# Two blocks of TensorE's stream change places in an attention kernel: the turn of the maxima and the sums of a group

## The chip, the cores and the metric

One core of a Trainium2 chip runs the whole kernel. The metric is the time of one execution on the device in microseconds; the median of several executions counts.

## What is computed

A gated block in two parts, for 16 sequences of 512 tokens with 512 features, in fp32. The first part is attention with 16 heads of 32 features, causal, of the normalised x over a context; the second is a channel mix (three matrix products with a shift by one token, a squared relu and a sigmoid).

```python
def _xattn(Q, K, V, mask, Wq, bq, Wk, bk, Wv, bv, Wo, bo):
    q, k, v = heads(Q @ Wq.T + bq), heads(K @ Wk.T + bk), heads(V @ Wv.T + bv)
    scores = jnp.einsum('bhqd,bhkd->bhqk', q, k) * SCALE
    scores = jnp.where(mask[:, None, None, :] == 0, -jnp.inf, scores)
    scores = jnp.where(causal[None, None], scores, -jnp.inf)
    attn = jax.nn.softmax(scores, axis=-1)
    return merge(jnp.einsum('bhqk,bhkd->bhqd', attn, v)) @ Wo.T + bo

x = x + jnp.tanh(g_xattn[0]) * _xattn(_layernorm(x), ctx, ctx, mask, ...)
x = x + jnp.tanh(g_ffn[0]) * _ffn(_layernorm(x), W_r, W_k, W_v, mu_r, mu_k)
```

## The kernel before, in words

The attention phase goes through 256 slots, one for each head of each sequence (16 slots a sequence, called a batch here), and 14 more to run out. `slot(i)` exists for each engine, and each engine runs through its own list of slots; semaphores alone tie them together. Several heads are in flight at once.

In slot i, TensorE does for head i the scores of the queries against the keys (`scores`, L844), in three portions: s0 (two products of 128 and 256 columns), s1 (384) and s2 (512), in two PSUM banks by turns. VectorE reads each portion and takes the maximum of each row (`maximum`, L697, four a slot). After an odd slot it splits the eight columns of maxima of two heads in a high and a low part (`split_maxima`, L705 and L707). In the even slot behind, TensorE turns them from columns to rows (`turn_maxima`, L853, a transpose into the bank `sum_ps`), ScalarE copies them out (`copy_maxima`, L518), and SP moves them by DMA into two rows of the stack `q_stack` (`stack_maxima`, L305).

With them TensorE makes, three slots behind, for head u = i - 3, the transposed scores less their maxima (`probabilities`, L867), again in three portions, p0, p1 and p2 (512, 384 + 128 and 256 columns), in two banks by turns. ScalarE takes their exponential (`exponent`, L531, three a slot) into a ring `probs` of five heads; GpSimd masks them (L383, L387) and adds them up in part (L394, L397).

Four heads are a group. In every fourth slot, from slot 8 on, TensorE makes the values of a group (`values`, L884, 32 products whose weights have 32 columns; four heads lie side by side in the columns of the array) and its sums, with ones as weights (L889, L892, L895, such products too, into `sum_ps`). The last of them raises `values_done`. In this document such a slot, i = 4m, is a group slot. The turn and the sums use the same bank: the sums wait until ScalarE has copied the turned maxima out (`max_copied`), and a turn waits until VectorE is through with the sums before (`refined`).

Behind `values_done` comes, in the order of ScalarE's list: the first exponential of the group slot (its place in the ring is the one that the values have just read), the logarithm of the sums (`log_sums`, L538), the second exponential, the reciprocal by an exponential of the negative logarithm (`invert_sums`, L542), the third exponential. VectorE then corrects the reciprocal (`refine`, L713 and L715), at the end of its list for the group slot, so ahead of the maxima of the next slot, and there scales the values (`normalise`, L720).

Between all these lie the projections of q, k, v and the output, each product split in three of high and low parts (`exact_product`, L54 to L56). A table written out by hand, `WORK`, says for each of the 16 slots of a batch which steps stand in each of three parts, where one step is three products of 512 columns:

```python
0: ("", "q1 2", ""),            # group slot; 4 and 8 alike, 12: ("", "q0+ 01", "")
1: ("q1 3,k1 0", "k1 12", "k1 3"),
2: ("v2 01", "v2 23", "v3 0"),  # 6 and 14 alike; 10: ("x0+", ...), four transposes
```

The waits of TensorE that matter here are written in the kernel as counts:

```python
# scores(u, c)
pe.wait_ge(scores_read, T * u + (-1, 0, 2)[c])
# probabilities(u, c)
pe.wait_ge(exp_done, 3 * u + c - 1)
# exponent(u, c), on ScalarE
act.wait_ge(values_done, (u - RING) // HG + 1)
```

So s2 of head u waits for two maxima of the same head, and p0, p1 and p2 wait for the exponential two portions earlier.

SP issues all DMA in one list: the stacks of q and k for later slots (L280, L289), the maxima (L305), loads of x, context and residual, and stores. The channel mix (from about 1475 us on) has lists of its own and isn't part of what is described here.

Of the kernel before, what the change touches and what calls it, by code (L numbers as in the profile page):

```python
# [83 lines left out]
def attention_phase(nc, lent, x, ctxT, mask, g_xattn, wqT, bq, wkT, bk, wvT, bv, woT, bo, x1, mask_bias, ffn_wT):  # L84
# [13 lines left out]
    HG = P // DH  # L98
    N = B * H
    LAG = 3  # L100
    VALUES = 8
# [14 lines left out]
    with ExitStack() as ctx:  # L116
# [130 lines left out]
        def k_stack_count(G):  # L247
            b, g = divmod(G, K)
            return 112 * b + (64 if g < 2 else 112)

        def value_block(b, g):
            return 0 if g < 2 else 1 + b % 2
# [579 lines left out]
        def _(pe):  # L832
            def scores(u, c):
                G, j = divmod(u, HG)
                n = G % 2
                if c == 0 and u % 2 == 0:
                    pe.wait_ge(q_stacked[n][j // 2], 48 * (G // 2 + 1))
                    pe.wait_ge(k_stacked[n][j // 2], k_stack_count(G))
                if u > 0 or c == 2:
                    pe.wait_ge(scores_read, T * u + (-1, 0, 2)[c])  # L840
                here = score_ps[(3 * u + c) % 2]
                for t in ((0, 1), (2,), (3,))[c]:
                    at = P if t == 1 else 0
                    last = nc.tensor.matmul(here[:, at:at + P * (t + 1)], q_stack[n][0:MASK_ROW + 1, j, P * t:P * t + P],  # L844
                                            k_stack[n][0:MASK_ROW + 1, j, 0:P * (t + 1)], start=True, stop=True)
                last.then_inc(scores_done, 1)

            def turn_maxima(q):
                pe.wait_ge(max_split, q + 1)
                ended = (2 * q + 1 - VALUES) // HG + 1  # L850
                if ended > 0:
                    pe.wait_ge(refined, ended)
                nc.tensor.transpose(sum_ps[0:2 * PAIR * T, 0:P], split_max[:].bitcast(F32), ident[:]).then_inc(max_turned, 1)  # L853

            def probabilities(u, c):

                G, j = divmod(u, HG)
                n = G % 2
                if c == 0 and u % 2 == 0:
                    pe.wait_ge(max_stacked[n][j // 2], 16 * (G // 2 + 1))  # L860
                if 3 * u + c >= 2:
                    pe.wait_ge(exp_done, 3 * u + c - 1)
                here = prob_ps[(3 * u + c) % 2]
                at = 0
                for k in PT_SETS[c]:
                    width = S - P * k
                    last = nc.tensor.matmul(here[:, at:at + width], k_stack[n][0:ROWS, j, P * k:P * k + P],  # L867
                                            q_stack[n][0:ROWS, j, P * k:S], start=True, stop=True)
                    at += width
                last.then_inc(probs_done, 1)  # L870

            def values(G):

                b, g = divmod(G, K)
                pe.wait_ge(summed, 2 * HG * (G + 1))
                pe.wait_ge(v_copied, T * (b + 1))
                if G > 0:
                    pe.wait_ge(normalised, G)
                if g == 1 and b + 1 < B:
                    pe.wait_ge(xt_low, T * (b + 2))  # L880
                for k in range(T):
                    for j in range(HG):
                        at = P * (g % 2) + DH * j
                        nc.tensor.matmul(value_ps[DH * j:DH * j + DH, P * k:S], v[:, value_block(b, g), k, at:at + DH],  # L884
                                         probs[:, (HG * G + j) % RING, PT_AT[k]:PT_AT[k] + S - P * k],
                                         start=(k == 0), stop=(k == T - 1), skip_group_check=True)
                pe.wait_ge(max_copied, min(2 * G + 4, N // 2))
                for j in range(HG):
                    nc.tensor.matmul(sum_ps[DH * j:DH * j + DH, 0:P], ones[:], probs[:, (HG * G + j) % RING, 0:P],  # L889
                                     start=True, stop=True, skip_group_check=True)  # L890
                for j in range(HG):
                    nc.tensor.matmul(sum_ps[DH * j:DH * j + DH, P:S], ones[:], prob_sum[:, (HG * G + j) % RING, :],  # L892
                                     start=True, stop=False, skip_group_check=True)
                for j in range(HG):
                    last = nc.tensor.matmul(sum_ps[DH * j:DH * j + DH, LATE:S], ones[:],  # L895
                                            probs[:, (HG * G + j) % RING, PT_AT[3]:PT_AT[3] + P],
                                            start=False, stop=True, skip_group_check=True)
                last.then_inc(values_done, 1)
# [51 lines left out]
            def transpose_x(b, m):  # L950
                if m != 1:
                    free_bank(f"x{m}", b)
                elif b > 0:
                    pe.wait_ge(normalised, K * (b - 1) + 1)
                pe.wait_ge(ln_applied, T * b + m + 1)
                for k in range(K):
                    last = nc.tensor.transpose(bank(f"x{m}")[:, P * k:P * k + P], tiles[:, m, P * k:P * k + P], ident[:])
                last.then_inc(xt_done, 1)
# [3 lines left out]
            def work(b, s, part):  # L962
                for piece in WORK[s][part].split(","):
                    if not piece:
                        continue
                    name, *steps = piece.split()
                    of = b + {"+": 1, "-": -1}.get(name[2:], 0)
                    if not 0 <= of < B:
                        continue
                    if name[0] == "x":  # L970
                        transpose_x(of, int(name[1]))
                    for k in (steps[0] if steps else ""):
                        project[name[0]](of, int(name[1]), int(k))

            def slot(i):
                b, s = divmod(i, H)
                u = i - LAG
                now, then = 0 <= i < N, 0 <= u < N
                if now:
                    scores(i, 0)  # L980
                if then:
                    probabilities(u, 0)
                if 2 <= i <= N and i % 2 == 0:
                    turn_maxima(i // 2 - 1)
                if i % HG == 0 and 0 <= i - VALUES < N:
                    values((i - VALUES) // HG)
                work(b, s, 0)
                if now:
                    scores(i, 1)
                if then:  # L990
                    probabilities(u, 1)
                if now:
                    scores(i, 2)
                work(b, s, 1)
                if then:
                    probabilities(u, 2)
                work(b, s, 2)
# [16 lines left out]
            for i in SLOTS:  # L1014
                slot(i)
# [439 lines left out]
```

## Time and profile before

| | |
|---|---|
| median of 3 runs | 2069.2 us (2066.35 to 2071.6) |
| the profiled execution | 2069.11 us |
| its span, first to last instruction | 2067.4 us |
| busy: TensorE, VectorE, GpSimd, ScalarE | 1943.2, 1355.8, 1298.9, 975.5 us |
| TensorE's granted clock over the span | 0.979 |

Read it so: TensorE is busy for 94% of the span, no other engine for more than 66%. The clock is given as a share of full speed. Idle time of the other engines costs nothing as long as TensorE doesn't wait for them; so the table alone doesn't tell what bounds a slot, the order of events does. Busy times of TensorE are those of pipelined products whose ends are modelled: the distance from start to start tells more than a length.

### The profile page before, as it was taken

The numbers are of one execution on the slowest core, as the hardware profiler recorded it, in microseconds if no ns is written. First come the engines' busy times: TensorE is split into PE (matmuls) and PEld (weight loads), VectorE is DVE, ScalarE is ACT, GpSimd is POOL, SyncE is SP. The second block draws the span as 40 slices with busy tenths as digits, with TensorE's granted clock in tenths as the row PEclk, the third lists the DMA queues.
The fourth block names the chain that finished last, engine by engine and source line by source line (L and its number), as shares of the span: only waits on it lengthen the run. The fifth ranks groups of instructions, "written<-read, shape, count | busy, mean of one in ns | idle before, by whom it ended". The sixth has DMA issues, their size and how long they took to land. (4 is left out here: it accounts for less than half of the span.)

```text
span 2067.4 us, 36565 instructions
## 1 busy us (share of the span) xinstructions
PE 1943.2 (94%) x11648; PEld 1499.7 (73%) x11648; DVE 1355.8 (66%) x3534; ACT 975.5 (47%) x1869; POOL 1298.9 (63%) x1829
## 2 busy tenths in 40 slices
PE   4999999999999999999999999994599999999999
PEld 3677777777777777777777777772388888888887
DVE  3776677766777767767677676765457566666663
ACT  3555555555555555555555454544233343434342
POOL 4566666666666666666666666556267777777770
PEclk9999999999999999999999999996799999999999
DMA  5545455454644545545554455443121313232221
GB/s 180 114 114 129 109 153 116 111 126 114 149 119 107 125 121 144 116 113 123 125 142 112 119 119 129 118 115 98 61 82 66 117 61 106 76 101 81 89 74 62
DMA packets 128665, 229.31 MB, mean 111 GB/s; under 512 B 18656, under 2 KB 20704, under 8 KB 127616
## 3 DMA queue, kind: packets, MB, share of 16 engines
q1 hardware_dynamic: 128512, 227.43, 42.2%
q8 instruction: 77, 1.26, 0.3%
q14 instruction: 76, 0.62, 0.1%
HBM read 92.06 MB, written 33.59 MB: 61 GB/s over the span
## 5 line engine op out<-in xcount | busy, mean ns | idle before, releaser
L697 DVE CUSTOM_DVE_ANT_0 score_ps<-score_ps,causal 128x128 f32<-128x128 f32 (+3 forms) x1024 | 489.2, 505 | 342.2 <-PE score_ps L844 340.8
L531 ACT ACTIVATE probs<-prob_ps 128x512 f32<-128x512 f32 (+1 forms) x768 | 399.2, 528 | 404.6 <-PE sum_ps L895 202.2
L844 PE MATMUL score_ps<-k_stack,q_stack 97*128 97x128 f32 (+3 forms) x1024 | 319.7, 353 | 20.8 <-DVE least L697 13.7
L867 PE MATMUL prob_ps<-q_stack,k_stack 100*128 100x512 f32 (+3 forms) x1024 | 284.7, 319 | 14.3 <-ACT probs L531 7.2
L383 POOL TENSOR_SCALAR_AFFINE_SELECT probs<-probs 128x256 f32<-128x256 f32 x256 | 110.2, 430 | 277.6 <-ACT probs L531 277.6
L394 POOL TENSOR_TENSOR prob_sum<-probs 128x384 f32<-128x384 f32 x256 | 261.2, 1020 | 0.0
L844 PEld LDWEIGHTS score_ps<-k_stack,q_stack 97*128 97x128 f32 x1024 | 188.9, 191 | 72.5 <-DVE least L697 30.8
L867 PEld LDWEIGHTS prob_ps<-q_stack,k_stack 100*128 100x128 f32 x1024 | 193.1, 192 | 37.7 <-DMA q_stack<-max_rows 9.5
L397 POOL TENSOR_TENSOR prob_sum<-prob_sum,probs 128x256 f32<-128x256 f32 x256 | 194.6, 760 | 36.7
L387 POOL TENSOR_SCALAR_AFFINE_SELECT probs<-probs 128x256 f32<-128x256 f32 x256 | 106.4, 415 | 175.6 <-ACT probs L531 175.5
L884 PE MATMUL value_ps<-probs,v 128*32 128x512 f32 (+3 forms) x2048 | 155.1, 444 | 12.3 <-POOL prob_sum L397 12.3
L1129 POOL TENSOR_SCALAR wk_low_room<-wk_low_room,ffn_moments,ffn_newton 128x512 f32<-128x512 f32 x56 | 163.6, 2930 | 2.9 <-POOL ffn_newton L80 2.8
L1148 POOL TENSOR_TENSOR kact_low<-square,kact_high 128x512 fp32r<-128x512 f32 x64 | 82.1, 1306 | 120.2 <-ACT kact_high L1196 120.2
L1286 DVE SCALAR_TENSOR_TENSOR square<-ffn_k_ps,relu 128x512 f32<-128x512 f32 x64 | 44.3, 692 | 160.0 <-ACT relu L1190 159.9
L697 DVE DVE_READ_ACCUMULATOR2_ANT least<- 128x1 f32 x1024 | 145.8, 142 | 0.0
L884 PEld LDWEIGHTS value_ps<-probs,v 128*32 128x32 f32 x2048 | 61.5, 111 | 103.4 <-issue 76.3
L54 PE MATMUL proj_ps<-cT_high,wk_high 128*128 128x512 f32 x256 | 102.2, 399 | 17.3 <-DVE wk_low L738 17.3
L1190 ACT ACTIVATE relu<-ffn_k_ps 128x512 f32<-128x512 f32 x64 | 38.3, 598 | 166.1 <-PE ffn_k_ps L56 166.1
L54 PE MATMUL ffn_k_ps<-mix_k_high,xT_high 128*128 128x512 f32 x256 | 105.6, 413 | 10.0 <-DVE mix_k_low L1272 10.0
L54 PE MATMUL proj_ps<-wo_high,attn_high 128*128 128x512 f32 x256 | 106.3, 415 | 8.0 <-issue 5.2
L54 PE MATMUL proj_ps<-wv_high,cT_high 128*128 128x512 f32 x256 | 104.5, 408 | 3.3 <-DVE xT_low L675 3.3
L54 PE MATMUL proj_ps<-xT_high,wq_high 128*128 128x512 f32 x256 | 102.2, 399 | 1.6 <-DVE staged_q_low L680 1.6
(144 smaller groups left out, 4879.7 us busy)
## 6 DMA issues: line engine op xcount, KB each, us to landing
k_stack<-staged_k_high SPq DMA_DIRECT2D x256, 128.0 KB
q_stack<-staged_q_high SPq DMA_DIRECT2D x256, 128.0 KB, 3.1
tiles<-in_x SPq DMA_DIRECT2D x16, 1024.0 KB, 5.6
k_stack<-staged_k_low SPq DMA_DIRECT2D x128, 128.0 KB
q_stack<-staged_q_low SPq DMA_DIRECT2D x128, 128.0 KB, 3.2
x_io<-in_x SPq DMA_DIRECT2D x16, 1024.0 KB, 6.9
x<-x_io SPq DMA_DIRECT2D x64, 256.0 KB, 3.3
wk_low_room<-x SPq DMA_DIRECT2D x16, 1024.0 KB, 5.6
```

The costliest lines, as they stand in the source:

```text
L54: nc.tensor.matmul(out, s_high, m_high, start=first and n == steps[0], stop=False)
L383: nc.gpsimd.affine_select(out=pair, in_=pair, compare_op=ALU.is_ge, fill=0.0, base=0, pattern=[[0, 2], [1, P]], channel_multiplier=-1).the ...
L387: nc.gpsimd.affine_select(out=pair, in_=pair, compare_op=ALU.is_ge, fill=0.0, base=0, pattern=[[0, 2], [1, P]], channel_multiplier=-1).the ...
L394: nc.gpsimd.tensor_tensor(total, here[:, P:S], here[:, PT_AT[1]:PT_AT[1] + LATE], ALU.add).then_inc(summed, 1)
L397: nc.gpsimd.tensor_tensor(total[:, P:LATE], total[:, P:LATE], here[:, PT_AT[2]:PT_AT[2] + 2 * P], ALU.add).then_inc(summed, 1)
L531: nc.scalar.activation(probs[:, u % RING, lo:hi], prob_ps[(3 * u + c) % 2][:, 0:hi - lo], ACT.Exp, scale=SCALE).then_inc(exp_done, 1)
L697: nc.vector.tensor_tensor_reduce(out=here, in0=here, in1=causal[:, LATE - P * t:S], scale=-1.0, scalar=3e38, op0=ALU.add, op1=ALU.min, acc ...
L844: last = nc.tensor.matmul(here[:, at:at + P * (t + 1)], q_stack[n][0:MASK_ROW + 1, j, P * t:P * t + P], k_stack[n][0:MASK_ROW + 1, j, 0:P ...
L867: last = nc.tensor.matmul(here[:, at:at + width], k_stack[n][0:ROWS, j, P * k:P * k + P], q_stack[n][0:ROWS, j, P * k:S], start=True, stop ...
L884: nc.tensor.matmul(value_ps[DH * j:DH * j + DH, P * k:S], v[:, value_block(b, g), k, at:at + DH], probs[:, (HG * G + j) % RING, PT_AT[k]:P ...
L1129: nc.gpsimd.tensor_scalar(x_in[:, m, :], x_in[:, m, :], moments[:, m, 0:1], newton[:, 1, m:m + 1], ALU.subtract, ALU.mult).then_inc(ln_app ...
L1148: nc.gpsimd.tensor_tensor(kact[1][:, k, :], square[:, k, :], kact[0][:, k, :].bitcast(F32), ALU.subtract).then_inc(kact_low, 1)
```

## The change

Two blocks change places in TensorE's list. The turn of the maxima stands behind the first share of projections of its even slot, or, in a group slot, where that share is empty, behind the values, instead of ahead of both. The sums of a group, a part of `values` before, become a function `sums` of their own, which is called behind s1, p1 and s2 instead of directly behind the values. No instruction is added or taken away, and the lists of the other engines stay as they are.

```diff
                         nc.tensor.matmul(value_ps[DH * j:DH * j + DH, P * k:S], v[:, value_block(b, g), k, at:at + DH],
                                          probs[:, (HG * G + j) % RING, PT_AT[k]:PT_AT[k] + S - P * k],
                                          start=(k == 0), stop=(k == T - 1), skip_group_check=True)
+
+            def sums(G):
+
                 pe.wait_ge(max_copied, min(2 * G + 4, N // 2))
                 for j in range(HG):
                     nc.tensor.matmul(sum_ps[DH * j:DH * j + DH, 0:P], ones[:], probs[:, (HG * G + j) % RING, 0:P],
...
                     scores(i, 0)
                 if then:
                     probabilities(u, 0)
+                grouped = i % HG == 0 and 0 <= i - VALUES < N
+                if grouped:
+                    values((i - VALUES) // HG)
+                work(b, s, 0)
                 if 2 <= i <= N and i % 2 == 0:
                     turn_maxima(i // 2 - 1)
-                if i % HG == 0 and 0 <= i - VALUES < N:
-                    values((i - VALUES) // HG)
-                work(b, s, 0)
                 if now:
                     scores(i, 1)
                 if then:
                     probabilities(u, 1)
                 if now:
                     scores(i, 2)
+                if grouped:
+                    sums((i - VALUES) // HG)
                 work(b, s, 1)
                 if then:
                     probabilities(u, 2)
```

## Rows read from the trace of the kernel before

**Rows 1.** Busy time by stretch: start:end, length, busy per engine, clock, DMA.

```profile
160.00:1420.00 1260.00, 1216.22 (x8191) 922.46 (x8193) 878.60 (x2656) 666.32 (x1325) 786.02 (x1250) 0.99 0.51 124
```

**Rows 2.** Waits from 160 to 1420 us: us in total, times, longest.

```profile
ACT probs L531 <- PE sum_ps L895: 186.0, 58, 3.3
...
PEld sum_ps L853 <- DVE split_max L707: 36.8, 48, 1.8
...
PEld score_ps L844 <- DVE least L697: 26.1, 59, 0.5
```

**Rows 3.** TensorE in time: start, length, operation, [idle before].

```profile
638.62 0.27 PE L853 MATMUL sum_ps<-ident,split_max 128*16 128x128 f32 x1
638.82 2.36 PE L884 MATMUL value_ps<-probs,v 128*32 128x512 f32 x32
641.00 0.40 PE L889 MATMUL sum_ps<-probs,ones 128*32 128x128 f32 x8
...
641.86 0.40 PE L895 MATMUL sum_ps<-probs,ones 128*32 128x128 f32 x8
642.19 0.45 PE L844 MATMUL score_ps<-k_stack,q_stack 97*128 97x384 f32 x1
...
643.00 0.39 PE L54 MATMUL proj_ps<-xT_high,wq_high 128*128 128x512 f32 x1
643.23 0.39 PE L55 MATMUL proj_ps<-xT_low,wq_high 128*128 128x512 f32 x1
...
644.11 0.48 PE L867 MATMUL prob_ps<-q_stack,k_stack 100*128 100x512 f32 x1
...
646.64 0.51 PE L844 MATMUL score_ps<-k_stack,q_stack 97*128 97x512 f32 x1 [0.26 <-DVE least L697]
```

**Rows 4.** ScalarE in time, the same group slot.

```profile
642.39 0.60 ACT L531 ACTIVATE probs<-prob_ps 128x512 f32<-128x512 f32 x1 [3.21 <-PE sum_ps L895]
...
643.36 0.60 ACT L531 ACTIVATE probs<-prob_ps 128x512 f32<-128x512 f32 x1
643.84 0.64 ACT L542 ACTIVATE inverse<-inverse 128x512 f32<-128x512 f32 x1
```

**Rows 5.** VectorE in time, the same group slot and the next.

```profile
644.51 0.70 DVE L713 TENSOR_TENSOR sum_ps<-sum_ps,inverse 128x512 f32<-128x512 f32 x1 [0.56 <-ACT inverse L542]
...
646.06 0.47 DVE L697 CUSTOM_DVE_ANT_0 score_ps<-score_ps,causal 128x256 f32<-128x256 f32 x1
```

**Rows 6.** TensorE in time around the turn, slots 2, 6, 12 and 14.

```profile
649.40 0.39 PE L867 MATMUL prob_ps<-q_stack,k_stack 100*128 100x512 f32 x1
650.80 0.28 PE L853 MATMUL sum_ps<-ident,split_max 128*16 128x128 f32 x1 [1.00 <-DVE split_max L707]
...
671.21 0.39 PE L867 MATMUL prob_ps<-q_stack,k_stack 100*128 100x512 f32 x1
671.90 0.28 PE L853 MATMUL sum_ps<-ident,split_max 128*16 128x128 f32 x1 [0.30 <-DVE split_max L707]
...
702.89 0.40 PE L867 MATMUL prob_ps<-q_stack,k_stack 100*128 100x512 f32 x1
703.38 0.28 PE L853 MATMUL sum_ps<-ident,split_max 128*16 128x128 f32 x1
...
715.39 0.40 PE L867 MATMUL prob_ps<-q_stack,k_stack 100*128 100x512 f32 x1
715.62 0.27 PE L853 MATMUL sum_ps<-ident,split_max 128*16 128x128 f32 x1
715.71 0.47 PE L54 MATMUL proj_ps<-wv_high,cT_high 128*128 128x512 f32 x1
```

**Rows 7.** Issues on SP in time, of slot 2: the maxima.

```profile
651.39 0.65 SPq L305 DMA_DIRECT2D q_stack<-max_rows  x1
```

**Rows 8.** DMA issues: operation, count, KB each, median us to landing.

```profile
q_stack<-staged_q_high SPq DMA_DIRECT2D x256, 128.0 KB, 3.1
...
mask_bias<-x_io SPq DMA_DIRECT2D x1, 32.0 KB, 1.6
```

## The prediction

> **What bounds the kernel now.** First the busy table by stretch. From 160 to 1420 us the kernel is in the steady part of the attention phase, and TensorE is busy in 1216.2 of 1260 us at a granted clock of 0.99, far ahead of the others [rows 1]. So only two things can move the time there: work added to or taken from TensorE's stream, and its gaps. The channel mix behind 1500 us isn't touched.
>
> Then the table of waits, for the gaps [rows 2]. TensorE's weight loads stood 36.8 us before the turned maxima (L853), 48 times, until VectorE had split them; that is what the change aims at. They also stood 26.1 us, 59 times, before a score product until VectorE had read earlier scores. 59 in 1260 us is once in four slots. And ScalarE waited 186.0 us, 58 times, 3.2 us each, for L895, the last sums of a group. That is once in four slots too, and it asks what hangs on those sums.
>
> Then one group slot in order of time. I count from z = 641.86, where the row of the last sums (L895) starts. TensorE: turn 638.62, values 638.82, sums 641.00, then s1, p1, s2 (scores 1, probabilities 1, scores 2) from 642.19 to 643.00, and the projections [rows 3]. ScalarE begins the group's first exponential at 642.39 = z + 0.53, when L895 is over; then logarithm, second exponential at 643.36 (0.60 long) and reciprocal at 643.84 (0.64 long) follow back to back, to 644.48 [rows 4]. VectorE waits for the reciprocal: its correction starts at 644.51, and only behind it comes the second maximum of the next slot, 646.06 to 646.53 [rows 5]. TensorE's s2 of that next slot needs it and starts at 646.64, after a gap that the row puts down to VectorE [rows 3]. **So from the sums to that s2 there is a fixed chain of 4.78 us (z to 646.64) over ScalarE and VectorE, and TensorE already waits at its end.** The next slot's p0 at 644.11 waits a little too: the second exponential, which frees its bank, ends at 643.96.
>
> **The change part by part.** Nothing is computed more or less; two blocks change places on TensorE.
>
> *Gain: the turn comes later.* In a slot 4m + 2 the six projection products (four transposes at slot 10) now stand ahead of the turn, in a slot 4m the values. From p0 to the turn is 0.23 us without a wait (715.39 to 715.62, slot 14), but 1.40 in slot 2, 0.69 in slot 6 and 0.49 in slot 12 [rows 6]. Saved: 1.17 + 0.46 + 0.26 = 1.89 us in a batch. The first and the last of the 16 batches have neither the same neighbours nor the same waits, so 15 count: **28.4 us**. Does the wait really end? In slot 2 the turn would be reached at 649.40 + 0.23 + 6 x 0.23 = 651.01; the split let it go at 650.80 [rows 6], 0.2 us before. Slots 6 and 12 have more room.
>
> *Cost: the sums come behind s1, p1, s2.* This block now lies ahead of z. Where it stood it took 0.81 us (642.19 to 643.00). At the spacing of a product with 512 columns, 0.23 us (643.00 to 643.23) [rows 3], its 384 + 512 + 512 columns would take 0.17 + 0.23 + 0.23 = 0.63; the other 0.18 is spent on getting out of the products with 32 columns of weights. The turn, before, took 0.20 to the values (638.62 to 638.82); ahead of s1 it should be near the 0.09 that it takes ahead of a projection [rows 3, 6]. I take 0.81 - 0.11 + 0.02 = **0.72 us** more from a group slot's start to z; the 0.02 is for one more switch, which no row shows by itself. Low end: 0.63 - 0.11 = 0.52. High end: the turn saves nothing, and going into the values and into the sums costs another 0.11 each, 0.81 + 0.22 = 1.03.
>
> Would the 0.72 be given back behind z, where the block is missing? **No: this is the step that decides.** TensorE would reach the next slot's p0 earlier, but the second exponential ends z + 2.10 as before, and s2 is let go z + 4.78 as before. ScalarE is idle before z and full from z + 0.53 to z + 2.6 either way. VectorE reads the maxima of s1 and s2 before z instead of behind it, but then waits for the same reciprocal. So the gap behind z grows by what the block took. Slot 12 has six projection products in the middle instead of three, but the same chain with a fourth link on ScalarE, so I count it alike. Group slots with scores behind them, and no transfer of the channel mix's weights ahead: 8, 12, ..., 248, that is 61. 61 x 0.72 = **43.9 us**.
>
> *What is queued behind the moved turn.* On ScalarE: copying the maxima, and behind that the slot's exponentials. In a slot 4m they wait for the sums anyhow; in 4m + 2 the first comes some 1.4 us later while the p2 that needs it has three to six products ahead of it: nothing. On GpSimd, masks and sums of the exponentials shift with them; values need them a slot later: nothing. The sums themselves wait for that copy. Turn to end of copy is about 0.6 us (650.80, and the transfer's issue at 651.39 [rows 6, 7]) while s1, p1, s2 lie between: 0.8, nothing. On SP's queue: the transfer of the maxima and, in 4m + 2, the K stack of the next group behind it, 1.4 us later but needed more than a slot later: nothing. The maxima's own transfer is tighter. In a slot 4m + 2 behind the turn stand s1, p1, s2 (0.63 to 0.81), nine products (2.07), p2 and the next s0 (0.3 together): p0 comes 3.0 to 3.2 us behind the turn, 2.4 to 2.6 behind the issue. No row shows the landing of these 8 KB; 32 KB to DRAM took 1.6 us, 128 KB to the same stack 3.1 [rows 8]. By size it is nearer the first: nothing, with up to 0.7 us a slot kept for a rival.
>
> *Sum.* 43.9 - 28.4 = **+15.5 us** on the profiled execution's 2069.1 us (span 2067.4 and 1.7 around it), which is the median of the runs (2069.2) to 0.1. **2084.6 us.** With the ends of the block's cost: 61 x 0.52 - 28.4 = +3.3 and 61 x 1.03 - 28.4 = +34.4, that is 2072 to 2103.
>
> *A rule against the row.* Behind the sums the block takes those 0.18 us more than its columns [rows 3]: a change from one kind of product to the other isn't free here. The Trainium skill, "TensorE: Matmul & The Clock Gate", section "Step-by-step: what each phase is for", says that weights are loaded while earlier products are in flight. By that rule the switches would be free and only the low end paid.
>
> **The rivals.** A measurement of this kernel tells about 0.3% (6.2 us) from no change.
>
> *Switches are hidden in the new places* (0.12): the low end, +3.3 us, 2072. For it: score loads between projections cost nothing now. Against it: the 0.18 us behind the sums. This is what the rule of the page named above would give.
>
> *Faster: the chain doesn't hang on the sums* (0.11). The place is VectorE's correction. If it is let go by something ahead of the sums, the moved block is taken out of TensorE's stream behind z and put in ahead at no loss, and only the 28.4 us stay, less 61 extra switches of 0.11: -21.7, 2047. It decides from the point where the correction starts earlier than z + 2.65; halfway is no change. For it: the turn's waits are large and plainly in the stream. Against: the logarithm reads the very bank that the sums write, and the code's exponential waits for the same count.
>
> *The maxima land late* (0.06). If the 8 KB need 3.1 us as the 128 KB do, p0 of the slot behind 4m + 2 waits 0.5 to 0.7, in three slots of a batch: 15 x 3 x 0.6 = +27 more, 2112.
>
> *The turn waits still* (0.04). VectorE is at its limit in slots 4m + 1; if half of the 28.4 stays, 2099.
>
> *The forecast* (0.67): the rest, 2073 to 2103, most of it over 2076.
>
> **How the numbers follow.** Slower by over 0.3%: 0.65 of the forecast, 0.05 of the hidden switches, 0.06 and 0.04: 0.80. Within 0.3%: 0.02, 0.07, and 0.03 of halfway: 0.12. Faster: 0.08. The range 2070 to 2101 takes the forecast with nearly all of its bounds, the hidden switches and the remaining wait, and leaves out the faster rival and the late maxima, under 2 in 10.
>
> **What the profile will show.** Right: no gap before the turn (L853) in slots 2, 6 and 12, and z about 4.5 us behind a group slot's start; z to the next slot's s2 still 4.8, with the waits of L844 for the maxima's reading (26.1 us now) up by some 35 to 45; ScalarE's wait for L895 up from 3.2 to about 4.5 us each. Wrong: a correction earlier than z + 2.65 (the faster rival), waits of L867 for the transfer from max_rows (late maxima), or waits of L853 that stay. A granted clock under 0.97 in the same stretch would be something that I haven't counted.

## The result, and the profile after

The changed kernel takes 2094.3 us (median of four runs, 2093.1 to 2094.9), the kernel before, beside it, 2067.8 us: ratio 1.0128, 95% interval 1.0115 to 1.014. **It is 26.5 us slower.** The forecast was +15.5 us, the range 2070 to 2101. The profiled execution's span is 2092.7 us, 25.3 more than before.

TensorE has as many instructions as before and the same share of busy time, 94%. The steady stretch of the attention, by stretch as in [rows 1]:

```profile
160.00:1420.00 1260.00, 1216.72 (x8095) 902.31 (x8094) 863.11 (x2615) 651.30 (x1304) 773.41 (x1236) 1.00 0.49 121
```

In the same time TensorE is as busy as before, 1216.7 against 1216.2 us, but gets through 8095 products instead of 8191. So busy time doesn't show the loss: a product that stands behind a wait or a switch has a longer row (0.50 us at 653.49 below, 0.39 to 0.40 for its neighbours). The waits from 160 to 1430 us (us in total, times, longest), to be held against [rows 2]:

```profile
DVE sum_ps L713 <- ACT inverse L542: 162.3, 58, 3.2
...
ACT probs L531 <- PE sum_ps L898: 101.5, 58, 1.8
...
PEld score_ps L844 <- DVE least L697: 34.6, 59, 1.0
...
PE prob_ps L867 <- ACT probs L531: 20.2, 44, 0.8
```

The turn's waits for the split are gone from the list. New is TensorE's wait for an exponential (L867), and VectorE's wait for the reciprocal is 2.8 us each, against 0.7 before (39.4 us in 58 waits): it reads the maxima ahead of it now and has nothing left to do. Now the same group slot as [rows 3 and 6], TensorE in order of time (start, length, operation, idle before); the sums have the lines L892, L895 and L898 here:

```profile
648.76 0.39 PE L867 MATMUL prob_ps<-q_stack,k_stack 100*128 100x512 f32 x1
...
649.08 2.36 PE L884 MATMUL value_ps<-probs,v 128*32 128x512 f32 x32
651.37 0.28 PE L853 MATMUL sum_ps<-ident,split_max 128*16 128x128 f32 x1
651.40 0.42 PE L844 MATMUL score_ps<-k_stack,q_stack 97*128 97x384 f32 x1
651.66 0.40 PE L867 MATMUL prob_ps<-q_stack,k_stack 100*128 100x384 f32 x2
651.90 0.44 PE L844 MATMUL score_ps<-k_stack,q_stack 97*128 97x512 f32 x1
652.27 0.42 PE L892 MATMUL sum_ps<-probs,ones 128*32 128x128 f32 x8
...
653.16 0.40 PE L898 MATMUL sum_ps<-probs,ones 128*32 128x128 f32 x8
653.49 0.50 PE L54 MATMUL proj_ps<-xT_high,wq_high 128*128 128x512 f32 x1
...
655.41 0.47 PE L867 MATMUL prob_ps<-q_stack,k_stack 100*128 100x512 f32 x1 [0.45 <-ACT probs L531]
...
657.94 0.50 PE L844 MATMUL score_ps<-k_stack,q_stack 97*128 97x512 f32 x1 [0.27 <-DVE least L697]
```

Two numbers are to be read off. From z, the start of the last sums (653.16), to s2 of the next slot (657.94) it is **4.78 us, to the hundredth what it was before** [rows 3]. And from p0 to z it is 4.40 us, against 3.47 before (0.23 from p0 to the turn [rows 6], then 638.62 to 641.86 [rows 3]): 0.93 more. Over the 62 group slots of each trace the medians are the same: p0 to z 3.47 before and 4.40 after, z to s2 4.78 in both. Behind slot 12 the chain is longer, 5.30 before and 5.29 after. The first exponential on ScalarE and the correction on VectorE:

```profile
653.69 0.60 ACT L531 ACTIVATE probs<-prob_ps 128x512 f32<-128x512 f32 x1 [1.75 <-PE sum_ps L898]
```

```profile
655.81 0.70 DVE L713 TENSOR_TENSOR sum_ps<-sum_ps,inverse 128x512 f32<-128x512 f32 x1 [2.67 <-ACT inverse L542]
```

The first exponential starts at z + 0.53, the correction at z + 2.65, as in [rows 4 and 5].

The slots' lengths, from the start of s0 to that of the next (median over twelve batches in the middle of the trace, us), with the mean length of a batch of 16, show where time went for this kernel and for all that follow (slots 3, 7, 11 and 15 stay within 0.04 us in all of them, slot 8 is like 0, and 5 and 9 are like 1 but for e1 and e6, where they are 5.38 and 4.90):

| kernel | 0 | 1 | 2 | 4 | 6 | 10 | 12 | 13 | 14 | batch |
|---|---|---|---|---|---|---|---|---|---|---|
| before | 5.64 | 5.38 | 6.03 | 5.65 | 5.40 | 5.61 | 6.63 | 5.87 | 4.92 | 86.7 |
| changed | 6.03 | 5.92 | 4.84 | 6.03 | 4.84 | 5.61 | 6.59 | 6.57 | 4.86 | 88.3 |
| e1 | 5.64 | 5.47 | 4.84 | 5.65 | 4.84 | 5.61 | 6.63 | 5.86 | 4.86 | 85.1 |
| e2 | 6.03 | 5.91 | 6.02 | 6.03 | 5.40 | 5.62 | 6.59 | 6.58 | 4.91 | 90.1 |
| e3 | 6.13 | 5.92 | 6.03 | 6.13 | 5.38 | 5.62 | 6.96 | 6.58 | 4.91 | 90.8 |
| e4 | 5.64 | 4.90 | 6.37 | 5.65 | 5.75 | 6.44 | 6.63 | 5.48 | 5.37 | 86.8 |
| e5 | 6.03 | 5.43 | 4.85 | 6.03 | 4.84 | 5.62 | 6.59 | 5.59 | 4.86 | 86.1 |
| e6 | 5.64 | 5.49 | 4.84 | 5.64 | 4.84 | 6.46 | 6.63 | 5.48 | 4.86 | 84.8 |
| e7 | 5.64 | 4.90 | 5.19 | 5.65 | 4.84 | 6.46 | 6.65 | 5.48 | 4.86 | 84.3 |
| e8 | 6.30 | 5.37 | 4.84 | 6.30 | 4.84 | 5.63 | 7.02 | 5.87 | 4.86 | 87.2 |
| e9 | 5.64 | 4.90 | 5.19 | 5.64 | 4.84 | 6.46 | 6.64 | 5.48 | 4.86 | 84.3 |
| e10 | 5.64 | 4.90 | 5.19 | 5.64 | 4.84 | 6.46 | 6.63 | 5.48 | 4.86 | 84.2 |
| e11 | 5.64 | 5.39 | 5.28 | 5.64 | 5.37 | 5.62 | 6.37 | 5.87 | 4.92 | 85.6 |
| e12 | 5.64 | 4.90 | 4.84 | 6.44 | 4.84 | 5.69 | 6.37 | 5.48 | 4.86 | 83.7 |

The change gains 1.19 us in slot 2, 0.56 in slot 6 and 0.06 in slot 14, and loses 0.92 to 0.93 in each pair of a group slot and the slot behind it (0 and 1, 4 and 5, 8 and 9), 0.66 in 12 and 13, where the turn's wait of 0.26 was inside.

### The profile page after: what moved, and what is told of

It is laid out like the page before. It is cut to its first block and busy times, and to the rows that moved or that the text cites. A ratio compares the mean times of both kernels' runs of the same rounds, so it can differ in the third digit from the quotient of the medians.

```text
span 2092.7 us, 36565 instructions
## 1 busy us (share of the span) xinstructions
PE 1961.2 (94%) x11648; PEld 1488.8 (71%) x11648; DVE 1354.7 (65%) x3534; ACT 972.4 (46%) x1869; POOL 1296.5 (62%) x1829
## 5 line engine op out<-in xcount | busy, mean ns | idle before, releaser
L531 ACT ACTIVATE probs<-prob_ps 128x512 f32<-128x512 f32 (+1 forms) x768 | 395.0, 527 | 271.3 <-PE prob_ps L867 158.7
L844 PE MATMUL score_ps<-k_stack,q_stack 97*128 97x128 f32 (+3 forms) x1024 | 320.1, 354 | 29.9 <-DVE least L697 14.8
L867 PE MATMUL prob_ps<-q_stack,k_stack 100*128 100x512 f32 (+3 forms) x1024 | 291.2, 325 | 34.9 <-ACT probs L531 28.0
L867 PEld LDWEIGHTS prob_ps<-q_stack,k_stack 100*128 100x128 f32 x1024 | 193.4, 192 | 74.7 <-issue 26.3
L844 PEld LDWEIGHTS score_ps<-k_stack,q_stack 97*128 97x128 f32 x1024 | 189.2, 191 | 71.9 <-DVE least L697 40.3
L397 POOL TENSOR_TENSOR prob_sum<-prob_sum,probs 128x256 f32<-128x256 f32 x256 | 194.6, 760 | 36.7
L713 DVE TENSOR_TENSOR sum_ps<-sum_ps,inverse 128x512 f32<-128x512 f32 x64 | 44.8, 700 | 195.4 <-ACT inverse L542 195.4
L518 ACT COPY max_rows<-sum_ps 16x128 f32<-16x128 f32 x128 | 32.5, 254 | 242.0 <-PE sum_ps L853 242.0
```

Of the source, the lines that this page charges most:

```text
L397: nc.gpsimd.tensor_tensor(total[:, P:LATE], total[:, P:LATE], here[:, PT_AT[2]:PT_AT[2] + 2 * P], ALU.add).then_inc(summed, 1)
L531: nc.scalar.activation(probs[:, u % RING, lo:hi], prob_ps[(3 * u + c) % 2][:, 0:hi - lo], ACT.Exp, scale=SCALE).then_inc(exp_done, 1)
```

## The experiments

The theory in one sentence: only the way from a group slot's start to its sums counts, because a chain of 4.8 us over ScalarE and VectorE hangs on them; and the turn's waits were really in TensorE's stream. Each run below takes one piece of it. The kernel before ran beside each of them, with medians of 2066.5 to 2067.0 us. An edit shifts the lines behind it by one or two, so L843 and L866 are in some of these kernels what L844 and L867 are before.

### The two parts of the change, each alone

**e1**, the turn late in slots 4m + 2, group slots untouched:

```diff
-                if 2 <= i <= N and i % 2 == 0:
+                if 2 <= i <= N and i % HG == 0:
                     turn_maxima(i // 2 - 1)
                 if i % HG == 0 and 0 <= i - VALUES < N:
                     values((i - VALUES) // HG)
                 work(b, s, 0)
+                if 2 <= i <= N and i % HG == 2:
+                    turn_maxima(i // 2 - 1)
```

> The kernel before with one part of the change: in the slots 4m + 2 the turn stands behind the first share of projections; the group slots stay as they were. Theory (the turn's waits were plainly in TensorE's stream, the loss came from the sums alone): slots 2, 6 and 14 are shorter by 1.19, 0.55 and 0.06 us as in the changed kernel, 1.80 us in each of 15 batches, 27 us in all, so about 2041 us, faster than both kernels. Rival (VectorE is the bound, and time won at the turn is lost again at the next group's correction or split): within 0.3% of the kernel before, with larger waits of the scores for the reading of the maxima.

Measured: 2043.9 us, ratio 0.9888 (0.9869 to 0.9906), **22.7 us faster than before**. The turn in slot 2 of this kernel:

```profile
640.90 0.40 PE L54 MATMUL proj_ps<-wv_high,cT_high 128*128 128x512 f32 x1
...
641.59 0.27 PE L853 MATMUL sum_ps<-ident,split_max 128*16 128x128 f32 x1
641.62 0.42 PE L844 MATMUL score_ps<-k_stack,q_stack 97*128 97x384 f32 x1
```

No idle time stands before the turn. Of the expected 27 us 4 are missing. Slot 1 has a wait in most batches that it didn't have before (waits of this kernel, 160 to 1400 us):

```profile
PEld prob_ps L867 <- DMA q_stack<-max_rows: 17.2, 16, 6.5
```

The longest of them, 6.5 us near the end of the attention phase, isn't new: the kernel before waits 6.3 us in the same slot. Of the other 15, 10.7 us in all, 13 are in slot 1, and slot 1 got longer in some batches: the maxima's transfer lands late there, which is one of the forecast's rivals in a single place. e7 comes back to it.

**e2**, the other part alone: as the changed kernel, with the turn of the slots 4m + 2 back ahead of the projections.

```diff
                 grouped = i % HG == 0 and 0 <= i - VALUES < N
+                if 2 <= i <= N and i % HG == 2:
+                    turn_maxima(i // 2 - 1)
                 if grouped:
                     values((i - VALUES) // HG)
                 work(b, s, 0)
-                if 2 <= i <= N and i % 2 == 0:
+                if 2 <= i <= N and i % HG == 0:
                     turn_maxima(i // 2 - 1)
```

> The other part of the change alone: in the group slots values, turn, s1, p1, s2, sums; in the slots 4m + 2 the turn stays ahead of the projections. Theory (fixed chain from the sums): 0.92 us more in 61 group slots, 0.26 less in 15 of them (the turn's wait in slot 12), +52 us, about 2120 us, and the waits before the turn in slots 2 and 6 stay at 1.0 and 0.3 us. Rival (only the extra switches on TensorE cost, some 0.3 us a group): +14 us, 2082 us.

Measured: 2120.7 us, ratio 1.0253 (1.0233 to 1.0272), +54 us. Parts and whole agree: 54 less the 27 that the slots of e1 gain is the change's 26.5; by e1's whole time, 22.7, it would be 31, and the transfer's waits in slot 1, of which the changed kernel has hardly any, stand between. The rival, switches alone, is out.

**e3**, the smaller edit: only the sums moved, all turns at their old places.

```diff
+                if 2 <= i <= N and i % 2 == 0:
+                    turn_maxima(i // 2 - 1)
                 grouped = i % HG == 0 and 0 <= i - VALUES < N
                 if grouped:
                     values((i - VALUES) // HG)
                 work(b, s, 0)
-                if 2 <= i <= N and i % 2 == 0:
-                    turn_maxima(i // 2 - 1)
```

> Only the sums moved behind s1, p1 and s2; all turns stay at their old places, ahead of the values. Theory: the way from a group slot's start to the sums is longer by the block (0.81 us) and about 0.1 for a switch, the chain behind them stays 4.8 us, 61 times: +55 us, about 2123 us. If the sums move costs clearly less than e2, the turn's new place behind the values is a cost of its own. Rival (switches alone): +6 to +15 us.

Measured: 2129.8 us, ratio 1.0298 (1.028 to 1.0317), +63 us, where +55 was expected, and 9 more than e2. The turn's place behind the values is a gain, not a cost: 0.10 us a group slot, and the wait of slot 12. The rows of a group slot show the price of each switch between the products with 32 columns of weights and the others:

```profile
664.37 0.39 PE L867 MATMUL prob_ps<-q_stack,k_stack 100*128 100x512 f32 x1
664.60 0.27 PE L853 MATMUL sum_ps<-ident,split_max 128*16 128x128 f32 x1
664.80 2.36 PE L884 MATMUL value_ps<-probs,v 128*32 128x512 f32 x32
667.09 0.44 PE L844 MATMUL score_ps<-k_stack,q_stack 97*128 97x384 f32 x1
667.38 0.40 PE L867 MATMUL prob_ps<-q_stack,k_stack 100*128 100x384 f32 x2
667.62 0.44 PE L844 MATMUL score_ps<-k_stack,q_stack 97*128 97x512 f32 x1
667.99 0.43 PE L892 MATMUL sum_ps<-probs,ones 128*32 128x128 f32 x8
...
668.87 0.40 PE L898 MATMUL sum_ps<-probs,ones 128*32 128x128 f32 x8
```

The values take 2.29 us to the next product (664.80 to 667.09) where they took 2.18 to the sums (638.82 to 641.00 [rows 3]): 0.11 for leaving the products with 32 columns of weights. s2 takes 0.37 to the sums (667.62 to 667.99) against 0.29 to a projection (642.71, where s2 began before, to 643.00): 0.08 for entering them. p0 to z is 4.50 us (664.37 to 668.87), 1.03 more than before; 61 times that is 62.8 us.

### Where the chain is held

**e4**, the kernel before, with VectorE's correction moved from ahead of the next slot's first two maxima to behind them. TensorE's list isn't touched.

```diff
-                if i % HG == 0 and 0 <= i - VALUES < N:
-                    refine((i - VALUES) // HG)
...
                 if i % HG == 1 and 0 <= i - VALUES < N:
+                    refine((i - VALUES) // HG)
                     normalise((i - VALUES) // HG)
```

> The kernel before with VectorE's correction of the reciprocal moved behind the first two maxima of the next slot, directly ahead of the scaling of the values; nothing on TensorE changes. Theory (s2 of the slot behind a group slot waits only because the correction stands ahead of two maxima): the gap of 0.42 us before that s2 is gone, 61 times, 20 to 26 us faster, 2042 to 2048 us; z to that s2 falls from 4.8 to about 4.35 us. Rival (the chain is bound on ScalarE or by VectorE's whole load, the order there doesn't matter): no change, and the waits turn up before the turn in slots 2 and 6.

Measured: 2069.4 us, ratio 1.0012 (1.0002 to 1.0022): **no gain**, if anything 0.1% slower. Theory and rival were each half right. The gap before s2 is gone everywhere (slot 1 from 5.38 to 4.90, slot 13 from 5.87 to 5.48), so s2 does wait because of the correction's place in the list. But slots 2, 6, 10 and 14 are longer by as much, as the rival had it. Its waits from 160 to 1420 us:

```profile
PEld sum_ps L852 <- DVE split_max L707: 70.3, 72, 1.8
...
PEld score_ps L843 <- DVE least L697: 0.5, 2, 0.4
```

26.1 us before the scores became 0.5, and 36.8 us before the turn became 70.3 [rows 2]. Counted from z, VectorE ends its split of the slot behind a group slot at the same time in either order, to 0.12 us (0.5 later in slot 9), and with the turn early TensorE waits for that end. z to s2 is 4.36 us now.

**e5**, the changed kernel with the same edit: there the turn is late.

> The changed kernel, with VectorE's correction behind two maxima of the next slot. Theory (the block of s1, p1, s2 was put ahead of a chain whose last link is that correction; with the turn late, nothing else waits in the place of it): the wait before s2 of the slot behind a group slot, 0.43 us over what TensorE needs, goes, but the wait of p0 for the second exponential stays: 61 x 0.43 = 26 us less than the changed kernel, about 2068 us. Rival (as in the kernel before with the same edit, the time is only handed on to another wait): no gain, 2094 us.

Measured: 2057.4 us, ratio 0.9957 (0.9942 to 0.9971): 37 us less than the changed kernel, and faster than the kernel before. The same edit that brought nothing there brings 37 us here, more than expected, because slot 13 is shorter by 0.98 us and not by 0.49 like slot 1. TensorE's list is the same in both, so these 37 us were waiting, not work. What is left is the wait of p0 for the second exponential:

```profile
640.97 0.47 PE L866 MATMUL prob_ps<-q_stack,k_stack 100*128 100x512 f32 x1 [0.45 <-ACT probs L531]
```

z is 638.72 in this slot, so p0 of the next slot starts at z + 2.25, as in the kernel before (641.86 to 644.11 [rows 3]) and in the changed one (653.16 to 655.41). The moved block is lost at this earlier link already: against e4, which has the same late correction, slots 0 and 1 are still 0.92 us longer (11.46 against 10.54). Only in slots 12 and 13, with more projections ahead of p0, is most of it given back (12.18 against 12.11, with the turn's wait of 0.26 us gone from the first).

**e8**, the changed kernel with the sums directly behind the turn, so that TensorE waits for the copy of the maxima, but z comes earlier.

```diff
                 if 2 <= i <= N and i % 2 == 0:
                     turn_maxima(i // 2 - 1)
+                if grouped:
+                    sums((i - VALUES) // HG)
...
                     scores(i, 2)
-                if grouped:
-                    sums((i - VALUES) // HG)
```

> The changed kernel, with the sums directly behind the turn and ahead of s1, p1 and s2, so that TensorE waits there for the copy of the turned maxima. Theory (only the way from a group slot's start to the sums counts, since the chain behind is fixed): that way is 2.84 us to the turn, 0.65 of waiting, 0.89 for the sums, 4.4 instead of 4.63: 61 x 0.24 = 15 us less than the changed kernel, about 2080 us, though the wait of 0.65 us is new. Rival (the sum of TensorE's waits counts): 0.65 x 61 = 40 us slower than the changed kernel.

Measured: 2076.1 us, ratio 1.005 (1.0033 to 1.0066), 18 us less than the changed kernel.

```profile
640.23 2.36 PE L884 MATMUL value_ps<-probs,v 128*32 128x512 f32 x32
642.52 0.28 PE L853 MATMUL sum_ps<-ident,split_max 128*16 128x128 f32 x1
643.14 0.43 PE L892 MATMUL sum_ps<-probs,ones 128*32 128x128 f32 x8 [0.34 <-ACT max_rows L518]
...
644.03 0.40 PE L898 MATMUL sum_ps<-probs,ones 128*32 128x128 f32 x8
...
648.81 0.51 PE L844 MATMUL score_ps<-k_stack,q_stack 97*128 97x512 f32 x1 [0.26 <-DVE least L697]
```

TensorE now takes 0.62 us from the turn to the sums (0.34 reported as idle), in every group slot, and the kernel is faster than with s1, p1 and s2 in that place. p0 to z is 4.12 us (median), 0.28 less than in the changed kernel; 61 times that is 17 us. z to s2 is 644.03 to 648.81, 4.78 once more. **A wait ahead of the chain's start that makes the start earlier is worth more than work that makes it later.** The rival, that the sum of TensorE's waits counts, is ruled out.

### Better than both

**e6** is e1 with the late correction, **e7** also issues the maxima's transfer ahead of the 1 MB load of x on SP:

```diff
+                if 2 <= i <= N and i % 2 == 0:
+                    stack_maxima(i // 2 - 1)
                 if has_next and s == 0:
                     load_x(b + 1)
...
-                if 2 <= i <= N and i % 2 == 0:
-                    stack_maxima(i // 2 - 1)
```

> Group slots as before, the turn late in the slots 4m + 2, and the correction behind two maxima. Each of these edits ends a wait that took the other's gain: theory, by the slot lengths of the two runs that had one edit each: 3.0 us less a batch than before, about 2022 us, with a rest of 0.6 us before the turn of slot 10 and waits for the maxima's transfer in slot 1. Rival (only the turn's gain stays): 2044 us.

> As e6, and SP issues the transfer of the maxima ahead of the 1 MB load of x in slot 0 (in e1 TensorE waited 17.2 us in 16 slots 1 for that transfer). Theory (the 8 KB land behind the 1 MB): the wait of p0 in slot 1 goes, and 3 to 12 us against e6. Rival (the transfer is late for another reason): as e6.

Measured: 2037.7 (ratio 0.9851, 0.9829 to 0.9872) and 2030.4 us (0.9823, 0.9806 to 0.9839). e6 misses its 2022 by 16 us: slot 1 is 5.49 instead of 4.90, and slot 10 is 6.46, 0.84 longer than before where 0.6 was allowed for. The two times are not clear of each other, since e6's four runs lie between 2031.0 and 2040.7; the slots tell more. e7 settles slot 1: with the transfer first it is 4.90 and its waits for the transfer are gone, so the 8 KB did stand behind the 1 MB. In e7 slot 2 is 0.35 us longer instead, with waits of the turn for the split.

**e9** puts the turn of slot 10 behind s2, **e10** also that of slot 2 behind p1.

```diff
                 work(b, s, 0)
-                if 2 <= i <= N and i % HG == 2:
+                if 2 <= i <= N and i % HG == 2 and s != 10:
                     turn_maxima(i // 2 - 1)
...
                     scores(i, 2)
+                if 2 <= i <= N and s == 10:
+                    turn_maxima(i // 2 - 1)
```

```diff
-                if 2 <= i <= N and i % HG == 2 and s != 10:
+                if 2 <= i <= N and s in (6, 14):
                     turn_maxima(i // 2 - 1)
...
                     probabilities(u, 1)
+                if 2 <= i <= N and s == 2:
+                    turn_maxima(i // 2 - 1)
```

> As e7, with the turn of slot 10, whose first share is only four short transposes, behind s2. Theory (in e7 slot 10 is 6.45 us, 0.8 over what TensorE needs, mostly the turn's wait for the split): 0.5 to 0.8 us less in 15 batches, 8 to 12 us, about 2020 us. Rival (VectorE is late for the whole slot, and s2 waits for it instead): as e7, 2030 us.

> As e9, with the turn of slot 2 behind p1. Theory (0.35 us of slot 2 are the turn's wait): 15 x 0.35 = 5 us less than e9, about 2015 us. Rival (the maxima then land behind p0 of slot 3, which is 2.8 us away): as e9 or slower, with waits of p0 for the transfer in slot 3.

Measured: 2031.8 and 2034.0 us (ratios 0.9831 and 0.9838), no better than e7. Both theories fell. e10's slot 2 is 5.19 as in e7 and e9: its wait stands before s2 now, for VectorE's reading, and not, as e10's rival had it, before p0 of slot 3 for the transfer. In e9's slot 10 the wait has moved to s2, as its rival said:

```profile
678.65 0.49 PE L843 MATMUL score_ps<-k_stack,q_stack 97*128 97x512 f32 x1 [0.58 <-DVE least L697]
```

VectorE is late as a whole there, and its row and GpSimd's beside it say why:

```profile
677.01 0.94 DVE L707 TENSOR_TENSOR split_max<-least,split_max 128x8 fp32r<-128x8 f32 x1
```

```profile
676.92 1.00 POOL L394 TENSOR_TENSOR prob_sum<-probs 128x384 f32<-128x384 f32 x1
```

An operation on eight columns takes 0.94 us and ends when GpSimd's sum, begun just before, ends. In the kernel before it was the same ahead of slot 2, whose turn waits most:

```profile
649.62 0.92 DVE L705 CAST split_max<-least 128x8 fp32r<-128x8 f32 x1
650.57 0.17 DVE L707 TENSOR_TENSOR split_max<-least,split_max 128x8 fp32r<-128x8 f32 x1
```

```profile
649.52 0.99 POOL L394 TENSOR_TENSOR prob_sum<-probs 128x384 f32<-128x384 f32 x1
```

**e11** tests that on the kernel before, **e12** on e9: in odd slots GpSimd starts its sums when the maxima are split.

```diff
                     mask_probs(i - LAG)
+                    if i < N and i % 2 == 1:
+                        pool.wait_ge(max_split, i // 2 + 1)
                     sum_probs(i - LAG)
```

> The kernel before, and in odd slots GpSimd starts adding up the exponentials (L394) only when VectorE has split the maxima. Theory (the split of slot 1 takes 0.92 us for eight columns because L394, 0.99 us, runs at the same time, and the turn of slot 2 waits for that split): the split falls to 0.2 us, the turn's wait in slot 2 from 1.17 to about 0.45 us, as in slot 6, 15 times: 11 us less, about 2056 us. Rival (the long split has another reason, or what GpSimd does later meets the next operation of VectorE instead): no change, or slower by the delay on GpSimd.

> As e9, with the same wait on GpSimd. Theory: the long split operations (0.94 us, in slots 1 and 9) fall to 0.2, slot 2 is shorter by up to 0.35 and slot 10 by up to 0.7 us, 15 us less than e9, about 2016 us. Rival: as e9, 2032 us.

Measured: e11 2050.3 us, ratio 0.9923 (0.9909 to 0.9936), 16 us faster by one wait more; e12 2022.9 us, ratio 0.9789 (0.9776 to 0.9803), **43.6 us faster than before, the best of all**. e11's split ahead of slot 2 and GpSimd behind it:

```profile
641.67 0.17 DVE L707 CAST split_max<-least 128x8 fp32r<-128x8 f32 x1
641.87 0.17 DVE L709 TENSOR_TENSOR split_max<-least,split_max 128x8 fp32r<-128x8 f32 x1
```

```profile
642.12 1.02 POOL L394 TENSOR_TENSOR prob_sum<-probs 128x384 f32<-128x384 f32 x1 [0.53 <-DVE split_max L709]
```

Slot 2 falls from 6.03 to 5.28 and slot 12 from 6.63 to 6.37. So in slot 2 three quarters of a microsecond of the wait that the change set out to hide was a clash of two other engines. e12 gains 9 us against e9 where 15 were expected, since its slot 4 has become 0.8 us longer, with waits of the turn for the split. Its trace shows what holds that split, GpSimd's addition of the residual (L402):

```profile
637.88 1.17 DVE L707 CAST split_max<-least 128x8 fp32r<-128x8 f32 x1
639.08 1.20 DVE L709 TENSOR_TENSOR split_max<-least,split_max 128x8 fp32r<-128x8 f32 x1
```

```profile
637.72 2.53 POOL L402 TENSOR_TENSOR x_io<-x_io,bo_gated 128x512 f32<-128x512 f32 x2
```

In e9 the same two operations take 0.34 and 1.21 us. No run moved this addition.

## Why the prediction was right, and where it was off

**The direction and the mechanism held.** "Would the 0.72 be given back behind z? No": z to s2 stayed 4.78 us, and e5 and e8 show by two different edits that the distance from z sets the pace. One thing in it was told too narrowly: the prediction took the correction and s2 for the link that decides, and of p0 it said that it waits a little. Behind a slot like 0, p0 starts at z + 2.25 in the kernel before, the changed one, e4 and e5 alike, and e5 against e4 shows that this link alone keeps the block from being given back there; in slots 12 and 13 it takes the correction. The faster rival, a chain that doesn't hang on the sums, is out: in the changed kernel the correction started at z + 2.65 again.

**The turn's gain** was forecast as 1.17, 0.46 and 0.26 us for slots 2, 6 and 12; the table has 1.19, 0.56 and, with 0.06 in slot 14, 2.07 in all: 31 us instead of 28.4. e1 alone brought 22.7, since a transfer took part of it back in slot 1; in the changed kernel the longer group slots leave that transfer time enough (2.5 us of such waits).

**The term that was mis-sized is the block's cost**, 0.72 us a group. It is 0.92. "I take 0.81 - 0.11 + 0.02" counted one more switch at 0.02 because no row showed one. But taking the values and the sums apart makes TensorE enter and leave the products with 32 columns of weights once more: 0.09 into the values (648.76 to 649.08 is 0.32, against 0.23), 0.11 out of them, 0.08 into the sums. Against that the turn costs only 0.03 behind the values, not 0.09. So 0.87 for the block (651.40 to 652.27, with the 0.08 in it), 0.09 + 0.11 around the values, 0.03 within the sums (0.89 instead of 0.86), and 0.17 less for the turn (0.03 instead of 0.20) make 0.93, and the slots' lengths have 0.92 to 0.93. 61 x 0.92 = 56.1, less 31.0 = **+25.1 us**; the spans differ by 25.3. The stated high end, 1.03, had these switches in; the value taken was too near the low one. The Trainium skill, "TensorE: Matmul & The Clock Gate", section "Step-by-step: what each phase is for", would give free switches as the prediction reads it, and these runs don't agree with that reading: whatever is loaded ahead, e3 pays 0.11 us out of the values and 0.08 into the sums. e3's own expectation, 0.1 for a switch, made the same mistake and was 8 us too low.

**Signs that were named.** No gap before the turn, z to s2 at 4.8: right. Wrong: "waits of L844 up by some 35 to 45", they rose by 8.5. The growth stands one step earlier on the same chain, at p0, which waits for the second exponential (20.2 us on TensorE, none of it before): the reason had been stated, its consequence for the table not drawn. ScalarE's wait didn't grow to 4.5 us either; it was cut in two, since its copy of the maxima now comes in the middle (1.75 us behind it).

**The other rivals.** Late maxima showed in slot 1 alone, in e1, e5 and e6, and not as general lateness: behind the turn in 4m + 2 there was time enough. The turn's waits didn't stay. What was called "VectorE is at its limit in slots 4m + 1" was right in e4, though in part of these slots a clash with GpSimd, not its own work, drew out the split.

## What to carry to other kernels

Before work is moved across a point, ask what hangs on that point on other engines: the products moved here were hidden behind nothing, since a chain of fixed length began right behind them, and even an idle engine would have been cheaper than later sums (e8). Measure the parts of a double change one by one: here one half alone is worth -23 us and the other +54. A wait that one wants to hide is worth asking for its cause first: a third engine's timing gave 16 us by one added wait (e11), and one edit (the late correction) brought nothing alone and 37 us beside a late turn.

## What the runs showed of the hardware

VectorE's small operation on SBUF operands, begun while GpSimd adds two SBUF operands, is over only with that addition: 0.92 us (before) and 0.94 us (e9) beside a 1.0 us operation, 0.17 us when GpSimd is kept away (e11), 1.17 and 1.20 us beside GpSimd's two additions of the residual (e12). The maxima of the scores, which take one operand from PSUM, keep their length beside GpSimd's sums: in the kernel before those of 384 columns have a median of 0.57 us in 88 cases with no GpSimd operation beside them and 0.57 us in 56 beside the second sum (L397). The Trainium skill, "SBUF — State Buffer", section "SBUF: two separate sides", says that VectorE and GpSimd share a pair of SBUF ports that one of them holds for a whole instruction while the other is blocked; these traces agree.

A change between products with full weights and products with 32 columns of weights costs TensorE about 0.1 us each way (0.11 and 0.08 in e3, 0.09 into the values in the changed kernel), with no idle time reported at the border; in the busy table it isn't seen. Which property of these products costs it, no run isolates.
